# Second attention layer: the first block's gram term as a rounded 256-column product, and a new order of a head's work on four engines

## The reference

```
p     = softmax(q k_t^T * scale)            # 512 x 508
text  = p v_t
qsem  = l2norm(p text_ehs)                  # 512 x 512 features
sem   = qsem . l2norm(ip_ehs)               # 512 x 4
fused = q k_ip^T * scale + 0.5 * sem
out   = text + (softmax(fused) * mask) v_ip
```

## Time and profile before

| | us |
|---|---|
| median of 3 runs | 1718.63 (1717.26 to 1721.88) |
| the profiled execution, its own time | 1711.14 |
| its span, first to last instruction | 1709.3 |
| TensorE matmul busy | 1585.5 (93%) |
| TensorE weight loads busy | 1212.0 (71%) |
| VectorE busy | 1272.5 (74%) |
| ScalarE busy | 1113.4 (65%) |
| POOL busy | 459.7 (27%) |

### The profile page before, as it was taken

The page is one execution under the profiler, slowest core; times in us unless marked ns, Lnnn a source line. Parts: engine busy times, 40 slices in busy tenths (PEclk is TensorE's granted clock), DMA queues, the critical chain, the costliest instruction groups (busy, mean ns, idle before and its releaser), DMA issues.

```text
span 1709.3 us, 32278 instructions
## 1 busy us (share of the span) xinstructions
PE 1585.5 (93%) x8608; PEld 1212.0 (71%) x8608; DVE 1272.5 (74%) x3548; ACT 1113.4 (65%) x2323; POOL 459.7 (27%) x1233
## 2 busy tenths in 40 slices
PE   7888999999988899999998899999999889999993
PEld 3554489999455459999855537999965544899991
DVE  2797378887788538888778935888877983688875
ACT  1797367775399537777449925777727982677760
POOL 0343023332044213223115402333303440233320
PEclk9999999999999999999999999999999999999997
DMA  9010310010411221000131022000031103000000
GB/s 312 24 37 14 111 58 21 18 34 2 123 38 36 60 83 37 18 18 30 40 97 37 28 69 92 19 18 18 25 111 35 37 19 111 15 19 19 22 17 15
DMA packets 47715, 82.81 MB, mean 48 GB/s; under 512 B 4868, under 2 KB 12308, under 8 KB 47640
## 3 DMA queue, kind: packets, MB, share of 16 engines
q1 hardware_dynamic: 44968, 76.77, 14.6%
q10 hardware_dynamic: 2672, 5.13, 0.8%
HBM read 41.49 MB, written 34.10 MB: 44 GB/s over the span
## 4 chain that ended last, share of the span: by engine, by line
PE 78%; ACT 12%; issue 5%; DVE 2%; DMA 1%; SPq 1%; ACTq 0%; POOL 0%; DVEq 0%
PE ps_w L938 45%; PE ps_t L938 12%; PE ps_s L938 12%; PE ps_b L938 7%; ACT probsT_high L522 5%; ACT probsT L530 5%; PE ps_m L938 2%; DVE row_max L729 1%; DMA q_slots<-out_all 1%; ACT probs L541 1%; ACT q_slots L515 1%; DMA q_slots<-probsT_low 1%; SPq L350 0%; ACT probs L618 0%; POOL probsT_low L433 0%
## 5 line engine op out<-in xcount | busy, mean ns | idle before, releaser
L522 ACT ACTIVATE probsT_high<-ps_t 128x512 fp32r<-128x512 f32 x640 | 382.6, 598 | 118.1 <-PE ps_t L938 114.2
L714 DVE TENSOR_TENSOR probsT_low<-probsT,probsT_high 128x512 fp32r<-128x512 f32 x560 | 394.7, 705 | 77.8 <-ACT probsT L530 68.7
L938 PE MATMUL ps_w<-gram,probsT_high 128*128 128x416 f32 (+2 forms) x1280 | 387.5, 314 | 0.0
L530 ACT ACTIVATE probsT<-ps_t 128x512 f32<-128x512 f32 x640 | 384.3, 600 | 0.0
L938 PE MATMUL ps_w<-gram_low,probsT_high 128*128 128x384 f32 (+2 forms) x1280 | 351.5, 303 | 0.0
L453 POOL TENSOR_SCALAR exp_bias<-row_max 128x1 f32<-128x1 f32 x320 | 128.0, 400 | 689.3 <-DVE row_max L772 689.3
L558 ACT ACTIVATE probs<-ps_s,exp_bias 128x508 f32<-128x508 f32 x320 | 220.3, 689 | 123.8 <-POOL exp_bias L453 79.9
L938 PE MATMUL ps_t<-q_slots,k_slots 98*128 98x512 f32 x640 | 259.7, 424 | 0.9
L938 PEld LDWEIGHTS ps_w<-gram_low,probsT_high 128*128 128x128 f32 (+1 forms) x1280 | 242.3, 189 | 11.0
L938 PEld LDWEIGHTS ps_w<-gram,probsT_high 128*128 128x128 f32 (+1 forms) x1280 | 240.8, 188 | 11.5
L938 PE MATMUL ps_s<-k_slots,q_slots 96*128 96x512 f32 x640 | 238.0, 414 | 10.2 <-DMA q_slots<-out_all 4.0
(11 more groups left out here) (166 smaller groups left out, 2024.5 us busy)
## 6 DMA issues: line engine op xcount, KB each, us to landing
q_slots<-parts_q SPq DMA_DIRECT2D x128, 96.0 KB
k_slots<-parts_k SPq DMA_DIRECT2D x128, 96.0 KB
parts_k<-probsT_high SPq DMA_DIRECT2D x16, 512.0 KB, 4.8
parts_k<-probsT_high SPq DMA_DIRECT2D x24, 256.0 KB, 4.2
parts_q<-probsT_low SPq DMA_DIRECT2D x8, 512.0 KB, 4.3
parts_q<-x_sb SPq DMA_DIRECT2D x8, 512.0 KB, 4.6
k_slots<-probsT_high SPq DMA_DIRECT2D x24, 128.0 KB, 3.9
parts_q<-probsT_low SPq DMA_DIRECT2D x12, 256.0 KB, 4.0
```

The lines of the kernel that those rows point to most:

```text
L522: nc.scalar.activation(probsT_high[1 - par][:, t, :], ps_t[:, t % 2, :], ACT.Exp, scale=SCALE)
L530: nc.scalar.activation(probsT[:, t, :], ps_t[:, t % 2, :], ACT.Exp, scale=SCALE).then_inc(pt_block[l], 1)
L714: nc.vector.tensor_tensor(probsT_low[1 - par][:, t, :], probsT[:, t, :], probsT_high[1 - par][:, t, :].bitcast(F32), ALU.subtract).then_in ...
L938: return nc.tensor.matmul(out, lhsT, rhs, start=start, stop=stop)
```

## The change

The first block's term `p G00 p^T` is computed another way. With `h` the rounded `p`, TensorE multiplies the rounded transposed exponentials `probsT_high` by a 256-column matrix, twice the rounded part of `G00` beside twice its remainder. VectorE sums both halves weighted by `p - h/2`. This gives `p G00 p^T` less a term in `(p - h)` squared. For that, ScalarE makes `h/2` of head g+1 in one operation on 128 x 512 elements (`half_rounded`), and POOL subtracts it in place from `probs` (`less_half_high`), behind its first bias operation. Four products of 256 columns don't fit in one bank, so they come in two pairs, the second ahead of gram 2, and `zb_done` counts two a head.

The order of a step becomes, for TensorE: first block 0 and 1, gram 0, maxima's rows, scores 0, gram 1, T 0, scores 1, T 1, first block 2 and 3, gram 2, scores 2, T 2, scores 3, T 3, gram 3. For ScalarE: half, shift, scores 0, T 0, scores 1, T 1, T 2, scores 2, T 3, scores 3. For VectorE: first block 0 and 1, used 0, max 0, used 1, max 1, low 0, first block 2 and 3, used 2, max 2, low 1, max 3, low 2, used 3, low 3. Two small tiles move into the memory of others (`ip_shift`, and `weighed` in `stat`).

```diff
@@ POOL, step1 @@
+                def less_half_high(of, head):
+                    pool.wait_ge(half_high_in, head + 1)
+                    pool.sem_inc(passed, 1)
+                    nc.gpsimd.tensor_tensor(probs[of][:, :, 0:P], probs[of][:, :, 0:P], half_high[:, :, :].bitcast(F32),
+                                            ALU.subtract).then_inc(less_half, 1)
...
+                        if c == 0 and transposed:
+                            less_half_high(1 - par, g + 1)
+                if transposed and not scores:
+                    less_half_high(1 - par, g + 1)
@@ ScalarE, step1 @@
+                def half_rounded(of, head):
+                    act.wait_ge(p_chunk, SC * (head + 1) + CREDIT)
+                    act.wait_ge(less_half, head)
+                    nc.scalar.activation(half_high[:, :, :], probs[of][:, :, 0:P], ACT.Copy, scale=0.5).then_inc(half_high_in, 1)
...
                 if transposed:
+                    half_rounded(1 - par, g + 1)
                     shift(b, 1, n, k)
...
                 for c in range(SC):
+                    if scores and c < 2:
+                        exps(c)
+                    if first and c == 1:
+                        gram_rows(b, 0)
+                    if second and c == 0:
+                        gram_rows(b, 3)
+                        v1_rows(b, 0)
                     if transposed:
                         expT(b, 1, n, par, c)
-                    if scores and c < 2:
+                    if second and c in (1, 2):
+                        v1_rows(b, c)
+                    if scores and c > 1:
                         exps(c)
-                    if second and c == 0:
-                        gram_rows(b, 3)
-                    if second and c < TB - 1:
-                        v1_rows(b, c)
-                if first:
-                    gram_rows(b, 0)
-                if scores:
-                    exps(2)
-                    exps(3)
@@ VectorE, step1 @@
+                def first_block_used(pair):
+                    dve.wait_ge(b_done, 2 * g + pair + 1)
+                    for i in range(2):
+                        c = 2 * pair + i
+                        last = nc.vector.tensor_tensor_reduce(out=weighed[i],
+                                                              in0=ps_b[:, 2 * P * i:2 * P * i + 2 * P].rearrange("p (a k) -> p a k", a=2),
+                                                              in1=probs[par][:, c, 0:P].unsqueeze(1).to_broadcast([P, 2, P]),
+                                                              scale=1.0, scalar=0.0, op0=ALU.mult, op1=ALU.add,
+                                                              accum_out=out[:, c, HO + 1:HO + 2])
+                    last.then_inc(zb_done, 1)
+                if use:
+                    dve.wait_ge(less_half, g + 1)
                     dve.wait_ge(out_moved, g - 1 + CREDIT)
+                    first_block_used(0)
...
                 for c in range(SC):
+                    if use and c == 2:
+                        first_block_used(1)
                     if use and c < 3:
                         products_used(c)
+                    if c == 3 and transposed:
+                        lowT(b, 1, n, par, 1)
                     if scores:
                         maxima(c)
...
-                    if use and c == 3:
-                        products_used(c)
-                    if transposed:
-                        lowT(b, 1, n, par, c)
...
+                    if c == 1 and transposed:
+                        lowT(b, 1, n, par, 0)
+                if transposed:
+                    lowT(b, 1, n, par, 2)
+                if use:
+                    products_used(3)
+                if transposed:
+                    lowT(b, 1, n, par, 3)
@@ VectorE, gram_lows @@
+                if i == 0:
+                    nc.vector.scalar_tensor_tensor(out=gram00[:, 1, :], in0=src[:, 0:P], scalar=2.0, in1=gram00[:, 0, :].bitcast(F32),
+                                                   op0=ALU.mult, op1=ALU.subtract)
@@ TensorE, step1 @@
+                def first_block(pair):
+                    pe.wait_ge(zb_done, 2 * g + pair + CREDIT)
+                    for i in range(2):
+                        c = 2 * pair + i
+                        last = mm(ps_b[:, 2 * P * i:2 * P * i + 2 * P], probsT_high[par][:, 0, P * c:P * c + P],
+                                  gram00[:, :, :].rearrange("p a k -> p (a k)"), True, True)
+                    last.then_inc(b_done, 1)
                 if use:
                     pe.wait_ge(pt_block[1], TB * g + 1 + CREDIT1)
-                    pe.wait_ge(zb_done, g + CREDIT)
-                    for c in range(SC):
-                        last = mm(ps_b[:, P * c:P * c + P], probsT[:, 0, P * c:P * c + P], gram00[:, :], True, True)
-                    last.then_inc(b_done, 1)
-                if transposed:
-                    pe.wait_ge(max_chunk, SC * (g + 2) + CREDIT)
-                    head_maxT(1, 1 - par)
+                    first_block(0)
...
                     gram_product(0)
                 if transposed:
-                    scoresT_of(1, g, k, 0)
+                    pe.wait_ge(max_chunk, SC * (g + 2) + CREDIT)
+                    head_maxT(1, 1 - par)
                 if scores:
                     scores_of(0)
...
                     gram_product(1)
                 if transposed:
-                    scoresT_of(1, g, k, 1)
+                    scoresT_of(1, g, k, 0)
                 if scores:
                     scores_of(1)
+                if transposed:
+                    scoresT_of(1, g, k, 1)
...
                 if use:
+                    first_block(1)
                     gram_product(2)
-                if transposed:
-                    scoresT_of(1, g, k, 2)
                 if scores:
                     scores_of(2)
+                if transposed:
+                    scoresT_of(1, g, k, 2)
...
-                if transposed:
-                    scoresT_of(1, g, k, 3)
                 if scores:
                     scores_of(3)
+                if transposed:
+                    scoresT_of(1, g, k, 3)
```

More of the change, by code:

```diff
@@ L122, in build @@
         ident_r = sb("ident_r", [P, P], F32R)
-        ip_shift = sb("ip_shift", [1, T])
         ones = sb("ones", [P, 1])
@@ L127, in build @@
         v1_sb = sb("v1_sb", [P, TB, C])
-        gram00 = sb("gram00", [P, P])
+        gram00 = sb("gram00", [P, 2, P], F32R)
         gram = [sb(f"gram{p}", [P, TB, GW], F32R) for p in range(2)]
@@ L141, in build @@
         probs = [sb(f"probs{p}", [P, SC, S]) for p in range(2)]
+        half_high = sb("half_high", [P, SC, P], F32R)
         exp_bias = [sb(f"exp_bias{p}", [P, SC]) for p in range(2)]
@@ L149, in build @@
         dump = sb("dump", [P, 16])
+        ip_shift = probsT[0:1, 0, :]
         heads_out = probsT[:, :, 0:C]
@@ L155, in build @@
         stat = sb("stat", [P, nd, 8])
+        weighed = [stat[:, 32 * i:32 * i + 32, :].rearrange("p n e -> p (n e)").rearrange("p (a k) -> p a k", a=2) for i in range(2)]
         root = sb("root", [P, nd + IPN])
@@ L213, in build @@
         p_chunk = sem("p_chunk")
+        half_high_in, less_half = sem("half_high_in"), sem("less_half")
         st_block = [sem(f"st_block{l}") for l in range(2)]
@@ L604, in gram_rows @@
                 diag = P if i < TB - 1 else P - IPN
-                dst = gram00[:, :] if i == 0 else gram[0][:, i, P * (i - 1):P * (i - 1) + diag]
-                nc.scalar.activation(dst, src[:, 0:diag], ACT.Copy)
+                dst = gram00[:, 0, :] if i == 0 else gram[0][:, i, P * (i - 1):P * (i - 1) + diag]
+                nc.scalar.activation(dst, src[:, 0:diag], ACT.Copy, scale=2.0 if i == 0 else 1.0)
                 nc.scalar.activation(gram[0][:, i, P * i - P + diag:GA], src[:, diag:T - P * i], ACT.Copy, scale=2.0)\
@@ L775, in step1 @@
                 out = head_out[par]
+                def first_block_used(pair):
[8 more added lines that the diff above has]
+                    last.then_inc(zb_done, 1)
                 if use:
-                    dve.wait_ge(b_done, g + 1)
-                    dve.wait_ge(p_chunk, SC * (g + 1) + CREDIT)
+                    dve.wait_ge(less_half, g + 1)
                     dve.wait_ge(out_moved, g - 1 + CREDIT)
-                    for c in range(SC):
[L781 to L784, removed]
+                    first_block_used(0)
                 def products_used(c):
@@ L817, in gram_lows @@
                 diag = P if i < TB - 1 else P - IPN
-                if i > 0:
+                if i == 0:
+                    nc.vector.scalar_tensor_tensor(out=gram00[:, 1, :], in0=src[:, 0:P], scalar=2.0, in1=gram00[:, 0, :].bitcast(F32),
+                                                   op0=ALU.mult, op1=ALU.subtract)
+                else:
                     cols = slice(P * (i - 1), P * (i - 1) + diag)
@@ L1137, in step1 @@
                 if use:
+                    first_block(1)
```

(10 more changed lines are left out.)

1 line of the change is left out of this document (removed).

## The result

The median went from 1717.95 us (4 runs, 1713.71 to 1721.88) to 1760.64 us (4 runs, 1758.40 to 1764.89), a ratio of 1.0246 (95% interval 1.0223 to 1.0268). The profiled execution took 1760.29 us, its span is 1758.5 us. It was forecast slower, at 1777 (range 1738 to 1815; the forecast's own case, without its rivals, 1765 to 1793).

A forecast was written before the change was run, and what follows sets the result against it. TensorE's work bound the old kernel; the new order makes gram 0 wait on a ScalarE chain, 11.14 us a head. 72 times +0.85 less 3.0 is +58 on 1711.14, 1769, plus 7.5 gives 1777 us, range 1738 to 1815.

The forecast's parts named there:

- the forecast's own case: Whole kernel: the longer head period in 72 places gives 1777 us, range 1765 to 1793; chance 0.64.
- 1.2 us forecast before G0: TensorE, second layer: gram 0 waits while a 4.20 us chain behind gram 2 outlasts 3.00 us of TensorE work.
- one of the signs that I had given for being wrong: TensorE, second layer: prediction wrong if the wait stands before T 3 or the gram product's low part instead of gram 0.
- TensorE's own sum: TensorE, one second-layer head: first-block products 0.48 instead of 0.85 us, so 9.92 us if nothing else waited.
- The period: Second-layer head: 6.94 us from gram 0 to gram 2's end plus the 4.20 us chain, 11.14 against 10.29.
- The sum: Whole kernel: 72 times +0.85 is +61.2 us, the other 8 heads -3.0, total +58.
- the fill steps: Steps before each batch's first head: reordered, put at 0, bounds -1 to +2 us a batch.
- a lag of T3 that does not count: TensorE: T 3 waits for ScalarE's exponentials of T 1 until 8.3 instead of 7.7; gram 3 still ends in time.
- my second rival: POOL's bias 2 isn't blocked: loop 10.72 us, +0.43 a head, kernel 1747 us; chance 0.12.
- The remainder: Whole kernel: total gain in time of +58 us on the profiled execution's 1711.14, giving 1769.
- the 7.5 us that I added as an offset: Whole kernel: the runs' median 1718.63 was 7.5 us above the profiled execution, so 1769 became 1777.
- The first-block use: VectorE, second layer: goes from 128 to 256 elements and takes 0.42 us.

The follow-up runs named there:

- b_pair1_pair3: The changed kernel with ScalarE's exponentials of T 1 ahead of scores 1, and of T 3 ahead of scores 2; 1687.97 us, ratio to the kernel before 0.9828.
- i_t3_first: b_pair1_pair3 with T 3 ahead of scores 3 on TensorE; 1682.57 us, ratio to the kernel before 0.9782.
- c_low1_late: The changed kernel with VectorE's low 1 behind max 3 instead of behind max 2; 1762.00 us, ratio to the kernel before 1.0261.

## Why the prediction was right

The forecast was slower, and the mechanism named was at work: pair 3 behind exp 2, exp 2 behind G2, and L1117's wait for all four pairs. It was not the whole of it. Moving pair 3 alone gave 21 us back, and only with pair 1 moved too came the whole loss and the term's gain. The direction and the length of the head were right. Where TensorE waits was right in part: of the 1.2 us forecast before G0, 0.34 stand there and 0.68 before T3, and a wait before T3 instead was one of the signs that I had given for being wrong. And 1760.64 lies in the whole range, but below my forecast's own 1765 to 1793.

- TensorE's own sum: 9.92 us a head was forecast and b_pair1_pair3 runs at 9.92. That they agree to the digit is luck. Rows m cost 0.07 less than the 0.31 in the sum, and the 0.08 of s3's wait make up for it: without that wait i_t3_first runs at 9.83. The products stepped at 0.12, as forecast.
- The period: 11.14 forecast, 11.00 in the head shown. Three terms were off and partly cancel. Rows m took 0.24 and not 0.31 (314.91 to s0 at 315.15), so the earlier trace rows had a transition in them. Used 2 to exp 2 took 2.03 and not 2.19, because bias 2 took 0.47 and not 0.63. TensorE restarted 0.13 behind pair 3 (323.93 to 324.06) and not 0.06. The sum is -0.07 - 0.16 + 0.07 = -0.16, against -0.14.
- The sum: the 72 distances add up to 791.6 us, before to 741.2. That is 50.4 more, 0.70 each, where 61.2 and 0.85 were forecast. The two profiled executions differ by 1760.29 - 1711.14 = 49.2. The rest, -1.2, is +2.0 before the first rows m of the program, where the change does nothing, and -3.2 in the first layers, the fill steps, the last two heads and what is behind them. For these -3.0 was forecast, with the fill steps at 0. The fill steps, the last heads and what follows them bring -0.8 a batch, and the traces do not part them, since m stands at another place in the step. The forecast had nothing for the 1 us of the load's issue in the first batch.
- What I called a lag of T3 that does not count (T3 from 7.7 to 8.3) was there: T3 started 8.31 behind G0. I did not see that behind pair 1 and pair 2 ScalarE itself reaches exp 2 just when bias 2 does. I had put ScalarE 0.2 ahead of bias 2's chain there (9.1 against 9.33). It had no such lead: pair 2's turn ended at 322.16, 0.04 behind the end of bias 2 at 322.12. The second chain was as long as the first. So an unblocked bias 2, my second rival, would have brought nothing: c_low1_late shows that, where I priced it at 0.42 a head.
- The remainder: 58 forecast, 49 between the profiled executions, 43 between the medians. The first step is the period. The second is the 7.5 us that I added as an offset: the profiled execution of before was its fastest (1711.14, the others 1713.71 to 1721.88), while after's (1760.29) lies at its median. So the offset did not carry over to the kernel after. The last section shows that such differences go with the granted clock.
- The first-block use cost 0.42 as forecast (mean 419 ns, 128x256), the half 0.63 for 0.60, the subtraction 1.29. VectorE kept up with no slack: used 2 started at 320.13, the 0.20 behind G2's end that the transfer needs, with its predecessor's accumulator read at 320.08.

## What to carry to other kernels

When an operation is put ahead of another on an in-order engine, write down for each what it waits for, and follow the one behind to whoever has a wait on it at the next step. A wait that was met 1.36 us early can become the end of the period without a line of it changed. And the exchange that a saving needs (here rows behind the gram product, then transposed scores behind the shift) can be right on one engine while the same exchange on another costs more than all of it brings: each engine's order is a change of its own and is worth a run of its own.

## What the runs showed of the hardware

**The blocked bias has no fixed length.** POOL's 128x1 operation took 0.63 us where VectorE's subtraction had started 0.13 before it (318.78 and 318.91), and 0.47 where it had started 0.27 before it (321.38 and 321.65); in both it ended 0.06 to 0.07 us behind the subtraction (319.54 against 319.47, 322.12 against 322.06). So it waits for the end of that instruction, and alone it takes 0.21 (316.64), as bias 2 does at 321.71 with low 1 late. That is the exclusion which the Trainium skill states ("SBUF — State Buffer", section "SBUF: two separate sides"); by it the price of a blocked operation is what is left of the other one, not a constant. In the other direction, POOL's subtraction of 1.29 us (316.81 to 318.10) ran beside used 1, which reads one operand from PSUM and one from SBUF, and max 1, and neither got longer (0.54 and 0.68 us). A low did not meet it in the heads read here, so what it would do to one was not seen.

**The ends of the program run at one clock or the other.** TensorE has nothing to do for 24.6 us before the last transposes, in every kernel. The last 14 us, first of the kernel after, then with both lows late:

```profile
1744.50:1758.50 14.00, 9.70 (x22) 2.94 (x20) 2.24 (x3) 1.19 (x2) 0.00 (x0) 0.95 0.14 47
```

```profile
1730.70:1744.70 14.00, 10.40 (x15) 2.62 (x14) 2.24 (x3) 0.00 (x0) 0.00 (x0) 0.74 0.14 47
```

The granted clock is 0.95 there and 0.74 here, on a mean between the levels of 2.4 and 1.2 GHz, and from the last transposes to the end it takes 15.9 us (1742.55 to 1758.5) against 20.5 (1724.22 to 1744.7). That is 4.5 us for the same work; of the other profiles four have 15.9 to 16.0 us and six 17.7 to 18.3. The opening differs too. The first rows m of the program start at 48.70 us in the profiled execution of before, with a granted clock of 1.00 from 30 to 40 us. In after they start at 50.74, with 0.83 there, and in the ten other profiles at 50.2 to 53.2, with 0.69 to 0.85. Over the kernel before the time goes with the clock between executions: its nine beside i_t3_first ran 1714.69 us at a mean granted clock of 0.989, 1717.55 at 0.987, 1720.41 at 0.986 and 1723.12 at 0.984, and the profiled one 1711.14 at 0.991. So a few microseconds between two medians can be the clock at the ends of the program. What decides which level the two ends get was not tried.
